# A LoRA gather that fetches both copies of a sequence in one DMA, with the operand's rows in the order copy, rank, sequence

## What is computed

```python
def _lora_linear(x, W, A, B, adapter_indices):
    base = jnp.einsum('bsd,df->bsf', x, W)
    Ai = A[adapter_indices]                      # rank 16
    Bi = B[adapter_indices]
    lora = jnp.einsum('bsr,brf->bsf', jnp.einsum('bsd,bdr->bsr', x, Ai), Bi)
    return base + lora
gate = _lora_linear(x, Wg, Ag, Bg, adapter_indices)    # 512 -> 2048
up   = _lora_linear(x, Wu, Au, Bu, adapter_indices)    # 512 -> 2048
h    = jax.nn.silu(gate) * up
x    = x + _lora_linear(h, Wd, Ad, Bd, adapter_indices)    # 2048 -> 512
x    = x + einsum('bct,bcd->bdt', x, weights[adapter_indices])
```

## Time and profile before

| | |
|---|---|
| median of 3 runs | 1218.6 us (1215.49 to 1220.42) |
| profiled execution | 1219.65 us |
| its span in the trace | 1218.0 us |
| mean granted TensorE clock | 0.982 of full speed |
| TensorE busy | 1163.6 us, 96% |
| first stage (last use of `bq`) | to about 822 us |

### The profile page before, as it was taken

How to read it: one execution, slowest core, us unless ns; L and a number is a source line. 1 busy time by engine, 2 the same in 40 slices (tenths; PEclk the granted TensorE clock), 3 DMA queues, 4 the chain that set the end, 5 groups by cost and what they waited for, 6 DMA issues and landing times.

```text
span 1218.0 us, 23035 instructions
## 1 busy us (share of the span) xinstructions
PE 1163.6 (96%) x6720; PEld 1034.8 (85%) x6720; DVE 913.6 (75%) x1578; ACT 539.3 (44%) x902; POOL 256.3 (21%) x405
## 2 busy tenths in 40 slices
PE   4889999999999997999999999998899999999998
PEld 3678888887888886888888788887899999999997
DVE  6776777876787787678887788888667766776775
ACT  4544444543444443344453344456344444444442
POOL 5223221112201012220101111011322221231230
PEclk8899999999999999899999999999999999999999
DMA  5597876688667589666759978868777777667781
GB/s 188 161 308 241 244 222 180 170 235 262 189 180 234 171 238 264 190 194 187 233 166 274 280 223 252 243 215 307 244 265 244 244 239 273 232 230 274 231 277 66
DMA packets 155583, 276.26 MB, mean 227 GB/s; under 512 B 28898, under 2 KB 97634, under 8 KB 155330
## 3 DMA queue, kind: packets, MB, share of 16 engines
q1 hardware_dynamic: 133104, 213.48, 57.5%
q0 software_dynamic: 21488, 59.66, 14.6%
q10 hardware_dynamic: 866, 1.66, 0.4%
HBM read 200.23 MB, written 74.45 MB: 226 GB/s over the span
## 4 chain that ended last, share of the span: by engine, by line
PE 73%; SPq 9%; DVE 5%; DMA 5%; issue 4%; ACT 3%; POOL 1%; POOLq 0%; DVEq 0%; ACTq 0%
PE ps L1368 12%; PE ps L1369 12%; PE ps L1370 12%; PE ps L1517 8%; PE ps L1519 8%; PE ps L1518 8%; PE ps L1380 7%; SPq L276 7%; DMA bq<-b_dram 2%; PE ps L1398 2%; DMA h_raw<-h_dram 1%; DMA xst<-xg 1%; SPq L245 1%; ACT xo_hi L602 1%; SPq L199 1%
## 5 line engine op out<-in xcount | busy, mean ns | idle before, releaser
L1368 PE MATMUL ps<-xo_hi,w_hi 128*128 128x512 f32 x896 | 359.3, 401 | 12.0 <-DVE w_lo L886 10.7
L1369 PE MATMUL ps<-xo_lo,w_hi 128*128 128x512 f32 x896 | 354.8, 396 | 0.0
L1370 PE MATMUL ps<-xo_hi,w_lo 128*128 128x512 f32 x896 | 351.8, 393 | 0.0
L1368 PEld LDWEIGHTS ps<-xo_hi,w_hi 128*128 128x128 f32 x896 | 171.4, 191 | 43.0 <-DVE w_lo L886 10.7
L1370 PEld LDWEIGHTS ps<-xo_hi,w_lo 128*128 128x128 f32 x896 | 170.4, 190 | 38.2
L473 POOL DMA_DIRECT2D h_dram<-hs x128 | 96.0, 754 | 487.3 <-DVE hs L1001 247.9
L886 DVE TENSOR_TENSOR hl<-h_raw,hh 128x1024 fp32r<-128x1024 f32 x112 | 137.0, 1223 | 79.0 <-ACT hh L602 77.6
L1380 PEld LDWEIGHTS ps<-t_st,bq 128*128 128x128 f32 x1024 | 158.5, 193 | 44.2 <-DMA bq<-b_dram 18.0
L1369 PEld LDWEIGHTS ps<-xo_lo,w_hi 128*128 128x128 f32 x896 | 171.1, 191 | 26.6
L1380 PE MATMUL ps<-t_st,bq 128*128 128x256 f32 x1024 | 166.2, 286 | 21.7 <-DMA bq<-b_dram 15.9
L602 ACT ACTIVATE hh<-h_raw 128x1024 fp32r<-128x1024 f32 x112 | 117.9, 1053 | 113.3 <-DMA h_raw<-h_dram 72.0
(11 more groups left out here) (153 smaller groups left out, 2188.0 us busy)
## 6 DMA issues: line engine op xcount, KB each, us to landing
bq<-b_dram SPq DMA_DIRECT2D x992, 64.0 KB, 2.6
h_raw<-h_dram SPq DMA_DIRECT2D x112, 512.0 KB, 5.3
h_dram<-hs POOLq DMA_DIRECT2D x128, 256.0 KB, 4.2
raw<-packed SPq DMA_DIRECT2D x58, 512.0 KB, 4.0
h_dram<-h_f SPq DMA_DIRECT2D x96, 256.0 KB, 3.9
ad_raw<-a_d SPq DMA_DIRECT2D x64, 128.0 KB, 2.1
xs<-x POOLq DMA_DIRECT2D x16, 512.0 KB, 5.8
y_out_dram<-xs POOLq DMA_DIRECT2D x30, 256.0 KB, 4.7
```

Source lines behind the costliest of these rows:

```text
L1368: pe.matmul(bank, st[0], mv[0], start=start and kk == 0, stop=False, skip_group_check=True)
L1369: pe.matmul(bank, st[0], mv[1], start=False, stop=False, skip_group_check=True)
L1370: m = pe.matmul(bank, st[1], mv[0], start=False, stop=kk == 1, skip_group_check=True)
```

## The change

The 128 rows of the operand are put in the order copy, rank, sequence: row = copy * 64 + rank * 4 + sequence, where it was copy * 64 + sequence * 16 + rank. This has four parts. `gather_a` writes its 16 columns per matrix four elements apart. `slot_mask` follows the new order. The 32 rows of one sequence, both copies, now lie four partitions apart from one end of `bq` to the other, so a single DMA writes them, and reads its 16 source rows twice, through a leading dimension of size 2 and step 0. And the counts that are waited for are halved.

```diff
-GATHER = SLOTS * 2 * 16
+GATHER = SLOTS * 16
...
-        aq = [at("aq", 200704, [P, KT * 2, QS, RANK])] + [at(f"aq{q}", 202752 + q * 2048, [P, KT * 2, QS, RANK])
+        aq = [at("aq", 200704, [P, KT * 2, RANK, QS])] + [at(f"aq{q}", 202752 + q * 2048, [P, KT * 2, RANK, QS])
...
-                for half in range(2):
-                    r = half * QR + (b % QS) * RANK
-                    sp.dma_start(bq_raw[r:r + RANK, b // QS, :, :],
-                                 b_gu[0, bass.ds(slot_numbers[b], 1)].rearrange("a r k c -> (a r) k c"))\
-                        .then_inc(bq_raw_in[2 * b // SLOTS], 16)
+                sp.dma_start(bq_raw[b % QS:P:QS, b // QS, :, :].rearrange("r k c -> r (k c)"),
+                             b_gu[0, bass.ds(slot_numbers[b], 1)].rearrange("a r k c -> a r (k c)").to_broadcast([2, RANK, PIECE * WB]))\
+                    .then_inc(bq_raw_in[2 * b // SLOTS], 16)
...
-                    for half in range(2):
-                        r = half * QR + (b % QS) * RANK
-                        sp.dma_start(bq[n % 2][r:r + RANK, b // QS, :, :].bitcast(F32).rearrange("r k c -> r (k c)"),
-                                     b_dram[piece_of(g, k), bass.ds(slot_numbers[g * SLOTS + b], 1)].rearrange("a r c -> (a r) c"))\
-                            .then_inc(bq_in[n % 4], 16)
+                    sp.dma_start(bq[n % 2][b % QS:P:QS, b // QS, :, :].bitcast(F32).rearrange("r k c -> r (k c)"),
+                                 b_dram[piece_of(g, k), bass.ds(slot_numbers[g * SLOTS + b], 1)].to_broadcast([2, RANK, PIECE * BC]))\
+                        .then_inc(bq_in[n % 4], 16)
...
-                    pool.tensor_copy(aq[q if g == 0 else 0][:, :, s, :], a_all[:, bass.ds(a, 1), :, :].rearrange("p a k r -> p (a k) r"))\
+                    pool.tensor_copy(aq[q if g == 0 else 0][:, :, :, s], a_all[:, bass.ds(a, 1), :, :].rearrange("p a k r -> p (a k) r"))\
...
-                act.wait_ge(bq_raw_in[pair], 16 * SLOTS)
+                act.wait_ge(bq_raw_in[pair], 16 * SLOTS // 2)
...
-        "slot_mask": (np.arange(P)[:, None] % QR // RANK == np.arange(QS)[None, :]).astype(np.float32),
+        "slot_mask": (np.arange(P)[:, None] % QS == np.arange(QS)[None, :]).astype(np.float32),
```

More of the change, by code:

```diff
@@ L1397, in lora_a @@
                     src = xst[(B11, B12, B21, B22)[2 * (k // 2) + q // 2]][:, (k % 2) * HALF:(k % 2 + 1) * HALF]
-                    m = pe.matmul(bank[:, 0:QT], a[:, k * 2:k * 2 + 2, :, :].rearrange("p u s r -> p (u s r)"),
+                    m = pe.matmul(bank[:, 0:QT], a[:, k * 2:k * 2 + 2, :, :].rearrange("p u r s -> p (u r s)"),
                                   src[:, n], start=k == 0, stop=k == KT - 1)
```

## The result

The changed kernel takes 1977.74 us (median of 4 runs, 1975.53 to 1979.07), the kernel before beside it 1218.66 us. The ratio is 1.623, with an interval of 1.620 to 1.627. The forecast was 2030 us, slower, in a range of 1820 to 2400.

What follows compares the result with a forecast made beforehand. TensorE was taken as the bound before, two DMA engines carrying all gathers after. 0.9 + 1615 (gathers) + 20.7 (last piece) + 395.6 (untouched rest) = 2032 us of span, predicted as 2030, range 1820 to 2400.

Steps and rivals of the forecast that it cites:

- The mechanism: Each gather's source has 2 outermost, its destination 32 rows, so two engines carry 64 KB each, fourteen nothing; chance 0.90.
- three landings: Tables' stores with 8 outermost landed after 5.3 and 6.1 us, against 4.2 and 4.7 with 128; called weak evidence.
- The landing of the last gather: First stage: 39.9 MB on each of two engines takes 1615 us, counted from the first DMA at 0.9 us.
- 24.7: GB/s assumed for each of the two engines, from fine slices of 0.25 us taken as busy for 95%.
- The 28.5 GB/s: Best rate per engine, from the three highest slices (451 to 459 GB/s); would give 1819 us in all.
- The row 15.8 GB/s for gathers alone: Rate per engine with only gathers running; would give 2788 us, thought unlikely.
- GpSimd's strided copies: 64 copies written four elements apart; first 16 could cost 13 us more or 3 us less, set to zero.
- SP is held: A full queue makes SP's weight loads and h stores behind the gathers late; needed only next piece, costed at nothing.
- the third rival: PE clock falls while TensorE idles in the first stage; mostly hidden, adds 0 to 20 us; no separate chance given.
- Sixteen engines in one DMA: All 16 engines (or 8) still carry each gather, waits go away: 1204 to 1220 us, likeliest 1208; chance 0.06.
- The rival of the dear issue: All engines carry, but a repeated source makes SP's issue dear: at 3.06 us each, about 1950 us; chance 0.02.
- a landing of tens of us: Sign of the forecast: a gather's landing rises from 2.6 us to tens of us, queued behind others.

Runs made afterwards that it cites:

- rank_outermost: Changed kernel with the gather source's loops exchanged, 16 ranks outermost and the repeat inside (fetches wrong ranks), raw gathers by two DMAs: 1206.5 us, 0.992 of the kernel before.
- two_copies_far: Changed kernel with two real copies of the table 4 MB apart, 2 outermost, no step 0, raw gathers by two DMAs: 1987.7 us, 1.635 of the kernel before.
- half_repeated: Changed kernel with only every second sequence fetched by the repeated source, the others and the raw gathers by two DMAs: 1443.4 us, 1.186 of the kernel before.
- three_quarters_repeated: Changed kernel with three of four sequences fetched by the repeated source, the fourth and the raw gathers by two DMAs: 1713.0 us, 1.408 of the kernel before.
- order_two_dmas: Changed kernel's row order, strided copies and mask, but every sequence fetched by two DMAs of 16 rows: 1317.6 us, 1.083 of the kernel before.
- two_copies_near: Changed kernel with the table stored twice, an adapter's copies adjacent, so one DMA reads 32 rows in one dimension: 1237.7 us, 1.018 of the kernel before.

## Why the prediction was right

**The mechanism.** It said that a DMA is dealt out along the outermost dimension of both its sides, by a number that divides both, here two; and it rested that on three landings. Now it rests on rank_outermost and two_copies_far, which differ from the changed kernel in that dimension or in the repeat alone, on the packets, of which two are always under way, on the line through half_repeated and three_quarters_repeated, and on the store whose packets run 8 at a time.

**The sum, term by term.** The landing of the last gather was forecast at 1616 us; the last piece was first used at 1554.0 us (PE's timeline). The bytes were right, the rate was low: 39.9 MB by then are 25.7 GB/s, not 24.7. The packets bear it out, with 4 KB in 159 ns, or 25.8 GB/s, and never fewer than two under way. The 28.5 GB/s from which the range took its lower end was no rate that an engine can be seen to have: it came from slices of 0.25 us, which count packets by their start, and the fastest packet of 4 KB in any of the traces took 156 ns, 26.3 GB/s. The 24.7 came from the same slices (18 of them with a mean of 374.5 GB/s, not 17 with 376, which changes it by 0.1), with a guess of 95% for their busy share. That the guess fell within 4% is in part luck. From first to last use of the last piece it took 22.2 us (20.7 forecast), with the granted clock at 0.88 between 1550 and 1580. The rest took 1976.1 - 1576.2 = 399.9 us (395.6). Two and four us more, and 62 less: 2034 became 1978. The row 15.8 GB/s for gathers alone was rightly put aside.

**Costs set to nothing.** GpSimd's strided copies have a median of 0.648 us for 0.472, 40.2 us in all for 36.1, and the first sixteen end before 28 us: free, as said. SP is held and its loads and stores are late with it; TensorE's long waits are for `bq` alone (701.4 us; the next is one of 10.4, and it was 10.7 before), so that too cost nothing. TensorE's clock fell to 0.76 in the first stage, TensorE's busy time rose from 1163.6 to 1228.5 us, and nearly all of it lies in time in which it would have waited, as the third rival had it.

**Rivals.** Sixteen engines in one DMA would have given 1208 by the forecast, and rank_outermost gives 1206.5. The rival of the dear issue was priced from rows of stores and loads of x (0.43 us), and none of them steps over partitions. The step itself makes it 0.50 at the least and 0.54 in the median. Against the 1.2 us that eight gathers may cost that was harmless. Against the (11.4 - 2) / 16 = 0.6 us that sixteen may cost, it is not: with the register work around it a gather takes 11.4 / 16 = 0.71 us of SP.

**What to look for** was put as a landing of tens of us. The view gives no landing for these gathers; the held issues and the 22.6 us waits were the sign.

## What to carry to other kernels

Before two DMAs are merged into one, look at the outermost dimension of both sides: if only a small number divides both, few engines carry the whole DMA, and the mean DMA share falls while the kernel slows. Put the repeat inside, or the rows in one dimension. And count what a queue pays for an issue, with its steps over partitions, before rows are spread for the sake of fewer issues.

## What was not expected of the hardware

- A step of 4 partitions between the SBUF rows of a DMA raises SP's issue from 0.315 at the least and 0.367 in the median to 0.495 and 0.536 us, with the same count of rows (order_two_dmas). With 32 rows in one dimension it is 0.472 (two_copies_near).
- A repeat of step 0 inside the rows is free: 128 KB land after 3.1 us, against 2.9 us for 32 separate rows (rank_outermost, two_copies_near).
- A DMA engine with 4 KB rows and idle neighbours takes 159 ns for a row, 25.8 GB/s, against 18.6 in the mean with all sixteen at work. A view in slices as short as a packet shows 27 or 55 GB/s instead, since it counts packets by their start.
- With two engines behind, SP was held in a single issue for up to 10.8 us, and with it everything behind it in SP's order: the loads of weights landed after 17.1 us, not 4.0.
- From GpSimd's queue the same DMA is on two engines as well, but on others each time (1570.1 us, not 1977.7).
